# A recommendation tower: a ring of three sample tiles, hot items among the second tile's products, and nine one-hot tables instead of ten

## The chip, the core and the metric

The kernel runs on one core of a Trainium2 chip. The metric is device time in microseconds of one execution. TensorE multiplies (PE; its weight loads are listed as PEld), VectorE (DVE) and ScalarE (ACT) copy and convert, GpSimd (POOL) issues the gathers, SyncE (SP) issues most other transfers.

## What is computed

For 2048 samples, 26 embedding rows of 128 numbers are looked up, each by its id in its own table. Seven tables have 1000 rows, ten 1250, eight 12500 and one 125000. With the dense row of the sample this makes 27 vectors; all 351 products of two of them, and the dense row behind them, go through three layers:

```python
e = jnp.stack([tbl_0[ids[:, 0]], ..., tbl_25[ids[:, 25]]], axis=1)
combined = jnp.concatenate([e, r_dense_x[:, None, :]], axis=1)
z = jnp.einsum('bfd,bgd->bfg', combined, combined)[:, _TRIU_I, _TRIU_J]
h = jnp.concatenate([z, r_dense_x], axis=1)
h = jnp.maximum(h @ W_top1 + b_top1, 0.0)
h = jnp.maximum(h @ W_top2 + b_top2, 0.0)
y = h @ W_top3
```

## The kernel before

The samples are worked through in 8 blocks of 256, each of two tiles of 128 samples. In `xt` (128 embedding elements on the partitions, samples and 32 feature slots along them) a block's vectors come together; it has room for one block.

**Cold tables.** Sixteen tables are gathered (POOL, line 388): one indirect DMA for each tile and table, 128 rows into `raw`, which has two buffers, so a tile's gather waits until the tile two before it is turned. Gathers go out in bursts of three (`BURST`), and a burst waits until the first two of the burst before have landed. TensorE turns them (`turn_rows`, line 405) in four groups of four tables into an `x_ps` bank, and ScalarE copies the bank into `xt` (line 561).

**Hot tables.** The ten smallest (seven of 8 chunks of 128 rows, three of 10) lie in SBUF, split into a rounded part `hot_hi` and a residue `hot_lo`. An item is one hot table for one block; it is cut into pieces of up to 5 chunks. VectorE makes the one-hot matrix of a piece by comparing ids with row numbers (`make_piece`, line 593) into a ring of three, TensorE multiplies each chunk by `hot_hi` and `hot_lo` (`hot_piece`, line 418, 256 columns, a rounded f32 type), and ScalarE copies the finished item into `xt` (line 530). While the tables arrive, ScalarE rounds each (line 523) and VectorE makes its residue (line 582). SP loads a table when the residue of the one four before it is made, and the wide list of ids of an item (128 copies of 256 ids) when the pieces of the item four before are made.

**Products of features.** `products(m)` (line 434), called gram or G below: eight fills for each tile, each four f32 products of 108 columns (two records each in the profile), in two banks that are copied by ScalarE and VectorE together (line 269). A tile's first fill waits for the last turn of the tile and for all hot items of the block.

**Tail.** For each block: `cols` (transposes of `gram`, copied to `z`), `zt` (transposes of `z`), `h1`, `h2`, `y`: the layers, in steps of two products (lines 459 to 495).

**The order** is written out once, as a list of steps that TensorE, ScalarE and VectorE all follow. `plan(h)` (line 110) gives a block: hot pieces from the third item on, the tail steps of the block before spread among them by the costs in `COVER`, and the first tile's turns; then the first tile's fills with the second tile's turns between them; then the second tile's fills with the next block's first two items (`EARLY`) after every second fill. Those two are copied to `xt` when it is free. The last block's tail stands alone. Five weight matrices are rounded and split (lines 571 and 613) beside fills 1, 3, 5, 7 and 9.

## Time and profile before

| | us |
|---|---|
| three runs | 480.33, 480.82, 482.65; median 480.82 |
| the profiled execution | 486.82 |
| its span, first to last instruction | 485.0 |
| TensorE products busy | 437.1 (90%) |
| VectorE busy | 310.4 (64%) |
| ScalarE busy | 230.2 (47%) |
| POOL busy | 247.8 (51%) |

The span cut into 40 equal slices; a digit is the busy share of a slice in tenths, PEclk the granted clock in tenths of full speed:

```profile
PE   1776669899998999999889999999999999999978
DVE  4998237875387735885469645885488745882441
PEclk9999679999999999999999999999999999999999
DMA  6789212322123312232122321232133312310000
```

Matmuls overlap in the pipeline, so the length of a record (some 280 ns) is longer than what it costs; the cost is the distance between two starts. The engines' idle time counts only where the engine is on the way to the end.

### The profile page before, as it was taken

Reading aid. Unit: us, or ns where it says so; the run is one execution under the profiler, and the core shown is the slowest. Engines: PE = TensorE matmul, PEld = TensorE weight load, DVE = VectorE, ACT = ScalarE, POOL = GpSimd, SP = SyncE. Lnnn points to the kernel's source line nnn. Section 1 sums busy time; section 2 is a strip of 40 time slices with the busy share of each in tenths; the row PEclk is TensorE's granted clock in tenths of the full one; section 3 lists DMA queues with packets and bytes.
Section 4 is the critical chain, followed back from the end, with each engine's and each line's share of the span. In section 5 each row is a group of like instructions: output and inputs, shape, how many; then the busy total and the mean of one; then the engine's idle time right before and its main releaser. Section 6 shows DMA issues by size and latency. Waiting matters only on the chain.

```text
span 485.0 us, 9121 instructions
## 1 busy us (share of the span) xinstructions
PE 437.1 (90%) x3464; PEld 413.9 (85%) x3464; DVE 310.4 (64%) x503; ACT 230.2 (47%) x731; POOL 247.8 (51%) x264
## 2 busy tenths in 40 slices
PE   1776669899998999999889999999999999999978
PEld 1665669899897999999889998989898989889966
DVE  4998237875387735885469645885488745882441
ACT  2643343644455453644545444644546453634643
POOL 3652665655655556455654656555565556461000
PEclk9999679999999999999999999999999999999999
DMA  6789212322123312232122321232133312310000
GB/s 229 222 258 160 57 45 58 81 70 72 48 63 75 81 51 57 70 82 73 44 66 78 73 65 55 70 76 78 39 72 80 80 55 56 72 49 18 1 1 0
DMA packets 23995, 36.20 MB, mean 75 GB/s; under 512 B 6185, under 2 KB 18097, under 8 KB 23952
## 3 DMA queue, kind: packets, MB, share of 16 engines
q1 hardware_dynamic: 14880, 18.03, 14.7%
q0 software_dynamic: 8192, 16.79, 12.8%
q10 hardware_dynamic: 880, 0.80, 0.5%
q8 instruction: 28, 0.46, 0.4%
q14 instruction: 15, 0.12, 0.1%
HBM read 35.59 MB, written 0.01 MB: 73 GB/s over the span
## 4 chain that ended last, share of the span: by engine, by line
PE 82%; DMA 7%; issue 4%; POOL 3%; DVE 2%; ACT 0%; POOLq 0%; ACTq 0%; DVEq 0%
PE x_ps L418 31%; PE gram_ps L434 24%; PE tail_ps L489 15%; DMA raw<-in_tbl,ids_sb 7%; PE x_ps L405 5%; POOL raw L388 3%; PE tail_ps L468 3%; PE tail_ps L459 2%; PE tail_ps L495 2%; DVE gram L269 1%; DVE onehot L593 1%; DMA ids_sb<-in_ids 0%; DVE z L278 0%; ACT gram L269 0%; DVE zt_lo L326 0%
## 5 line engine op out<-in xcount | busy, mean ns | idle before, releaser
L388 POOL DMA_INDIRECT raw<-in_tbl,ids_sb x256 | 246.9, 964 | 190.9 <-DMA raw<-in_tbl,ids_sb 94.6
L593 DVE TENSOR_TENSOR onehot<-ids_wide,row_ps 128x1024 fp32r<-128x1024 int32 (+1 forms) x160 | 202.6, 1298 | 41.2 <-PE x_ps L418 32.3
L418 PE MATMUL x_ps<-onehot,hot_hi 128*128 128x256 f32 x688 | 180.1, 297 | 22.2 <-DVE onehot L593 20.2
L418 PE MATMUL x_ps<-onehot,hot_lo 128*128 128x256 f32 x688 | 171.4, 283 | 0.0
L418 PEld LDWEIGHTS x_ps<-onehot,hot_hi 128*128 128x128 f32 x688 | 131.3, 191 | 26.5 <-issue 11.9
L434 PE MATMUL gram_ps<-xt 128*128 128x108 f32 x1024 | 134.2, 284 | 7.3 <-DVE gram L269 5.8
L434 PEld LDWEIGHTS gram_ps<-xt 128*128 128x128 f32 x1024 | 126.9, 199 | 13.6 <-ACT gram L269 7.6
L418 PEld LDWEIGHTS x_ps<-onehot,hot_lo 128*128 128x128 f32 x688 | 131.6, 191 | 0.0
L269 DVE COPY gram<-gram_ps 32x104 f32<-32x104 f32 x256 | 68.6, 268 | 90.2 <-PE gram_ps L434 86.3
L269 ACT COPY gram<-gram_ps 32x104 f32<-32x104 f32 x256 | 60.2, 235 | 88.7 <-PE gram_ps L434 80.1
L530 ACT COPY xt<-x_ps 128x256 f32<-128x256 f32 x80 | 50.4, 633 | 50.1 <-PE x_ps L418 42.0
L405 PE MATMUL x_ps<-ident,raw 128*128 128x128 f32 x256 | 39.9, 280 | 9.3 <-issue 3.9
L561 ACT COPY xt<-x_ps 128x512 f32<-128x512 f32 x64 | 38.4, 600 | 13.8 <-PE x_ps L405 12.4
L405 PEld LDWEIGHTS x_ps<-ident,raw 128*128 128x128 f32 x256 | 30.5, 146 | 10.3 <-issue 8.6
L302 ACT ACTIVATE h_hi<-tail_ps,b_sb 128x256 fp32r<-128x256 f32 x32 | 15.2, 474 | 37.7 <-PE tail_ps L489 28.9
L489 PE MATMUL tail_ps<-zt_hi,weights_hi 118*128 118x256 f32 (+2 forms) x96 | 31.5, 353 | 0.0
L278 ACT COPY z<-tail_ps 64x104 f32<-64x104 f32 (+12 forms) x195 | 26.4, 209 | 6.3 <-PE tail_ps L459 3.9
L331 DVE TENSOR_TENSOR h_lo<-h,h_hi 128x256 fp32r<-128x256 f32 x32 | 13.7, 428 | 24.4 <-ACT h L303 15.7
L489 PE MATMUL tail_ps<-zt_hi,weights_lo 118*128 118x256 f32 (+2 forms) x96 | 25.6, 291 | 0.0
L468 PE MATMUL tail_ps<-ident,z 64*118 64x64 f32 (+3 forms) x128 | 14.8, 240 | 6.0 <-issue 2.9
L489 PE MATMUL tail_ps<-dense_sb,w1d_sb 128*128 128x256 f32 x64 | 19.9, 393 | 0.0
L468 PEld LDWEIGHTS tail_ps<-ident,z 64*118 64x118 f32 (+3 forms) x128 | 10.5, 139 | 10.8 <-issue 5.2
(36 smaller groups left out, 279.0 us busy)
## 6 DMA issues: line engine op xcount, KB each, us to landing
ids_wide<-in_hot_ids SPq DMA_DIRECT2D x80, 128.0 KB
raw<-in_tbl,ids_sb POOLq DMA_INDIRECT x256
hot_in<-in_tbl SPq DMA_DIRECT2D x7, 512.0 KB, 6.8
hot_in<-in_tbl SPq DMA_DIRECT2D x3, 640.0 KB, 6.6
dense_sb<-in_dense_t ACTq DMA_DIRECT2D x6, 128.0 KB
weights_in_place<-in_w SPq DMA_DIRECT2D x1, 512.0 KB
dense_sb<-in_dense_t SPq DMA_DIRECT2D x2, 128.0 KB
weights_in_place<-in_w SPq DMA_DIRECT2D x1, 256.0 KB
```

The costliest lines, as they stand in the source:

```text
L269: last = copy(gram[rows, :, per_fill * i:per_fill * (i + 1)], src)
L278: last = copy(z[rows, :, pair_start[q]:pair_start[q] + feats - 1 - q], src)
L302: nc.scalar.activation(h1_hi[:, j, :], ps[:, 0:BLOCK], ACT.Relu, bias=bias).then_inc(h1_rounded, 1)
L388: nc.gpsimd.indirect_dma_start(out=raw[k][:, f, :], out_offset=None, in_=tables[f], in_offset=bass.IndirectOffsetOnAxis(ap=ids_sb[:, t, f: ...
L405: last = nc.tensor.transpose(ps[:, c * P:(c + 1) * P], raw[k][:, f, :], ident[:, :])
L418: last = nc.tensor.matmul(ps, table[:, chunk_at[j] + c, :], onehot[:, p % RING, c - a, :], start=(c == 0 and table is hot_hi), stop=(c == ...
L434: last = nc.tensor.matmul(gram_ps[m % 2][:, col:col + QUAD * feats], xt[:, b:b + QUAD, :].rearrange("p b f -> p (b f)"), xt[:, b:b + QUAD, ...
L468: last = nc.tensor.transpose(ps[0:of.stop - of.start, s * groups_block:(s + 1) * groups_block], z[rows, s, of], ident[rows, rows])
L489: last = nc.tensor.matmul(ps[:, 0:BLOCK], weights, moving, start=(n == 0), stop=(n == len(products_of) - 1))
L530: copy(xt[:, :, nf + j], x_ps[fill_no["hot", it] % len(x_ps)][:, 0:BLOCK]).then_inc(x_copied, 1)
L561: copy(xt[:, b:b + P, fs[0]:fs[-1] + 1], src).then_inc(x_copied, 1)
L593: nc.vector.tensor_tensor(onehot[:, p % RING, 0:n, :], ids_wide[:, it % IDS, :].unsqueeze(1).to_broadcast([P, n, BLOCK]), row_no[chunks[it ...
```

## The change

It has several parts. `HOT` is 9: one 1250-row table goes over to the gathers, so a tile has 17 gathers in five groups of 3, 3, 4, 3 and 4. `xt` is a ring of three tiles (`XT`); `to_xt` makes a copy in two where it wraps around. Items of block 0 are for one tile each, later ones for a block; a piece holds up to 1024 columns of one-hot matrix (`PIECE`), so 8 chunks of one tile are one piece, and 4 chunks of a block. The 10-chunk items become pieces of 5 and 5 for a tile, of 3, 3 and 4 for a block.

The order in block 0: tile 0's nine items with its turns, its eight fills with an item of tile 1 after each, tile 1's last item and turns. In later blocks: the next block's first item, which is held in its bank until the first tile's products have been made; the first tile's eight fills; the second tile's turns among the item pieces that follow; then the second tile's eight fills with one hot piece after each; then the remaining items with the turns of the next first tile. The tail of a block is spread from the end of its second tile's fills to the start of the next block's. Among fills VectorE makes one piece per step, none before the first. SP loads with two tables ahead instead of three (`LOADS_AHEAD`), and four more id lists stand before the weights in its queue. The weight splits stand at fills 11 to 15. `h1_lo` takes the place of `h1`.

```diff
-HOT = 10
+HOT = 9
 RAW = 2
 DENSE = 2
 RING = 3
-PIECE = 5
-EARLY = 2
+PIECE = 4
 BURST = 3
+XT = 3
+ROUNDS_AHEAD = 2
 COVER = {"cols": 2.0, "zt": 1.0, "h1": 0.2, "h2": 0.15, "y": 0.25}
 COVER_STAGE = 2.5
 COVER_START = 1.5
-TAIL_OVER = 3
-LOADS_AHEAD = 3
+LOADS_AHEAD = 2
...
-    items = blocks * nh
+    items = [(j, t, 1) for t in range(tiles_block) for j in range(nh)]
+    items += [(j, h * tiles_block, tiles_block) for h in range(1, blocks) for j in range(nh)]
     pieces, item_end = [], []
-    for it in range(items):
-        n = chunks[it % nh]
-        count = -(-n // PIECE)
-        cut = [i * n // count for i in range(count + 1)]
+    for it, (j, _, n) in enumerate(items):
+        count = -(-chunks[j] * n * P // (PIECE * BLOCK))
+        cut = [i * chunks[j] // count for i in range(count + 1)]
         pieces += [(it, cut[i], cut[i + 1]) for i in range(count)]
         item_end.append(len(pieces))
     item_start = [0] + item_end[:-1]
...
+    last_item = [max(it for it, (_, first, n) in enumerate(items) if first <= t < first + n) for t in range(tiles)]
+    def hot_pieces(t):
+        of = [p for p, (it, _, _) in enumerate(pieces) if items[it][1] == t]
+        return [[("hot", p)] for p in of]
+    def with_turn(slots, t, ends):
+        for g in range(n_turn):
+            slots[ends[-(-(g + 1) * len(ends) // n_turn) - 1]].append(("turn", t, g))
+        return slots
+    def item_ends(slots):
+        return [i for i, slot in enumerate(slots) if slot[-1][0] == "hot" and slot[-1][1] + 1 in item_end]
+    def gram_slots(t, hot=()):
+        return [[("gram", t * n_gram + i)] + [step for slot in hot[i * len(hot) // n_gram:(i + 1) * len(hot) // n_gram]
+                                              for step in slot] for i in range(n_gram)]
...
+    slots = hot_pieces(0)
+    slots = with_turn(slots, 0, item_ends(slots)[-n_turn:])
+    tail_from, tail_to = [], []
+    for h in range(blocks):
+        t = h * tiles_block
+        hot = hot_pieces(t + tiles_block) if h + 1 < blocks else []
+        if h == 0:
+            second = hot_pieces(1)
+            slots += gram_slots(t, second[:n_gram])
+            rest_slots = second[n_gram:]
+            slots += with_turn(rest_slots, t + 1, item_ends(rest_slots))
+            lead = 0
+        elif hot:
+            held = item_end[pieces[hot[0][0][1]][0]] - hot[0][0][1]
+            slots += hot[:held] + gram_slots(t)
+            slots[-1].append(("held", pieces[hot[0][0][1]][0]))
+            lead = n_gram
+            ends = item_ends(hot[held:lead])[:-1]
+            slots += with_turn(slots[-1:] + hot[held:lead], t + 1, [0] + [end + 1 for end in ends])[1:]
+            tail_to.append(len(slots))
+        else:
+            slots += gram_slots(t) + with_turn([[] for g in range(n_turn)], t + 1, list(range(n_turn)))
+            lead = 0
+            tail_to.append(len(slots))
+        slots += gram_slots(t + 1, hot[lead:lead + n_gram])
+        tail_from.append(len(slots))
+        if hot:
+            rest_slots = hot[lead + n_gram:]
+            slots += with_turn(rest_slots, t + tiles_block, item_ends(rest_slots))
+    held_items = [step[1] for slot in slots for step in slot if step[0] == "held"]
...
+            before.setdefault(tail_from[h] + min(int(at * n / span[-1]), n - 1), []).append(("tail", h, key, part))
+        for i, steps in before.items():
+            slots[i][:0] = steps
+    order = [step for slot in slots for step in slot]
...
+        for n, step in enumerate(order):
             if step[0] == "hot":
                 used = step[1]
             end = min(used + RING + 1, len(pieces))
+            coming = [s[0] for s in order[n + 1:] if s[0] in ("gram", "hot")][:1]
+            if step[0] == "gram":
+                end = min(end, nxt + 1)
+            elif coming == ["gram"]:
+                end = nxt
...
-        xt = sb("xt", [P, BLOCK, SLOTS])
+        xt = sb("xt", [P, XT * P, SLOTS])
...
-        onehot = sb("onehot", [P, RING, PIECE, BLOCK], F32R)
+        onehot = sb("onehot", [P, RING, PIECE * BLOCK], F32R)
...
-        h1 = sb("h1", [P, m1, BLOCK])
...
+        with nc.sbuf_tensor("h1", [P, m1, BLOCK], F32) as h1:
+            pass
...
+        weights_at_gram = range(gram_block - len(weight_parts), gram_block)
...
+        def to_xt(copy, first, n, feature, src):
+            at = first % XT
+            runs = [(0, n)] if at + n <= XT else [(0, XT - at), (XT - at, n)]
+            for a, b in runs:
+                place = (first + a) % XT * P
+                last = copy(xt[:, place:place + (b - a) * P, feature], src[:, a * P:b * P])
+            return last
...
-                if j == EARLY:
-                    dense_load(0)
+            dense_load(0)
+            for it in range(nh, nh + IDS):
+                ids_load(it)
...
-                h, i = divmod(m, gram_block)
-                if i % n_gram == 0:
-                    t = h * tiles_block + i // n_gram
-                    pe.wait_ge(x_copied, max(fill_no["turn", t, n_turn - 1], fill_no["hot", h * nh + nh - 1]) + 1)
-                    pe.wait_ge(dense_copied, h + 1)
+                t, i = divmod(m, n_gram)
+                if i == 0:
+                    pe.wait_ge(x_copied, max(fill_no["turn", t, n_turn - 1], fill_no["hot", last_item[t]]) + 1)
+                    pe.wait_ge(dense_copied, t // tiles_block + 1)
                 for done in (gram_act, gram_dve):
                     reach(pe, done, m - 1)
                 for g in range(per_fill):
-                    b = (i * per_fill + g) * QUAD
+                    b = t % XT * P + (i * per_fill + g) * QUAD
...
-                if j == 0:
+                to_xt(copy, first, n, nf + j, x_ps[fill_no["hot", it] % len(x_ps)]).then_inc(x_copied, 1)
+                if j == nh - 1 and first % tiles_block == 0:
+                    h = first // tiles_block
                     act.wait_ge(dense_in[h % DENSE], (h // DENSE + 1) * 16)
-                    copy(xt[:, :, nf + nh], dense_sb[h % DENSE][:, :]).then_inc(dense_copied, 1)
-
-            for j in range(EARLY):
+                    to_xt(copy, first, tiles_block, nf + nh, dense_sb[h % DENSE]).then_inc(dense_copied, 1)
+            for j in range(ROUNDS_AHEAD):
...
-                    if what[0] + 1 == item_end[it]:
-                        if it >= nh and it % nh < EARLY:
-                            waiting.append(it)
-                        else:
-                            hot_copy(it)
-                elif kind == "xt free":
-                    if waiting:
-                        act.wait_ge(gram_full, (what[0] + 1) * gram_block)
-                    for it in waiting:
+                    if what[0] + 1 == item_end[it] and it not in held_items:
                         hot_copy(it)
-                    waiting = []
+                elif kind == "held":
+                    hot_copy(*what)
...
+                    if what[0] in weights_at_gram:
                         act.wait_ge(weights_in, n_weights * 16)
-                        hi, _, src = weight_parts[what[0] // 2]
+                        hi, _, src = weight_parts[weights_at_gram.index(what[0])]
                         copy(hi, src).then_inc(weights_rounded, 1)
```

## Rows read from the trace of the kernel before

**Rows 1.** Busy time by stretch: PE, PEld, DVE, ACT, POOL, granted clock, DMA share, GB/s.

```profile
0.00:48.50 48.50, 27.35 (x188) 24.62 (x188) 40.45 (x36) 20.29 (x26) 22.17 (x26) 1.00 0.80 217
48.50:72.80 24.30, 16.31 (x87) 15.57 (x88) 7.23 (x20) 9.02 (x25) 15.87 (x17) 0.70 0.19 51
72.80:485.00 412.20, 393.42 (x3191) 373.75 (x3189) 262.74 (x448) 200.93 (x682) 209.73 (x222) 0.99 0.23 59
```

**Rows 2.** Who TensorE waited for, 120 to 450 us: us in total, times, longest.

```profile
PE gram_ps L434 <- DVE gram L269: 5.8, 9, 1.2
PE x_ps L418 <- DVE onehot L593: 3.0, 2, 1.6
```

**Rows 3.** Chain that ended last, from the page: shares of the span by engine.

```profile
PE 82%; DMA 7%; issue 4%; POOL 3%; DVE 2%; ACT 0%; POOLq 0%; ACTq 0%; DVEq 0%
```

**Rows 4.** Timeline of POOL's gathers: start, length in us, instruction, idle before and releaser.

```profile
12.16 1.43 POOL L388 DMA_INDIRECT raw<-in_tbl,ids_sb  x1 [5.49 <-DMA raw<-in_tbl,ids_sb]
...
19.42 0.97 POOL L388 DMA_INDIRECT raw<-in_tbl,ids_sb  x1 [2.43 <-DMA raw<-in_tbl,ids_sb]
...
43.07 0.94 POOL L388 DMA_INDIRECT raw<-in_tbl,ids_sb  x1 [0.30 <-issue]
...
48.54 0.95 POOL L388 DMA_INDIRECT raw<-in_tbl,ids_sb  x1 [3.27 <-DMA raw<-in_tbl,ids_sb]
...
53.03 0.94 POOL L388 DMA_INDIRECT raw<-in_tbl,ids_sb  x1 [1.04 <-DMA raw<-in_tbl,ids_sb]
```

**Rows 5.** Timeline of VectorE in the first stage, one table and the next.

```profile
11.55 1.22 DVE L582 TENSOR_TENSOR hot_lo<-hot_in,hot_hi 128x1024 fp32r<-128x1024 f32 x1
12.69 2.35 DVE L593 TENSOR_TENSOR onehot<-ids_wide,row_ps 128x1024 fp32r<-128x1024 int32 x2
14.95 1.22 DVE L582 TENSOR_TENSOR hot_lo<-hot_in,hot_hi 128x1024 fp32r<-128x1024 f32 x1
```

**Rows 6.** Timeline of TensorE in the first stage: transposes, first fill, fills at 70.60.

```profile
22.95 0.60 PE L405 MATMUL x_ps<-ident,raw 128*128 128x128 f32 x4
...
49.00 1.14 PE L434 MATMUL gram_ps<-xt 128*128 128x108 f32 x8 [0.68 <-ACT xt L561]
...
70.60 4.38 PE L434 MATMUL gram_ps<-xt 128*128 128x108 f32 x24
```

**Rows 7.** Timeline of TensorE, one-hot products of a steady block, ten intervals apart.

```profile
251.07 0.28 PE L418 MATMUL x_ps<-onehot,hot_lo 128*128 128x256 f32 x1
...
252.27 0.28 PE L418 MATMUL x_ps<-onehot,hot_lo 128*128 128x256 f32 x1
```

**Rows 8.** DMA issues of one list of ids and one table, from the page.

```profile
ids_wide<-in_hot_ids SPq DMA_DIRECT2D x80, 128.0 KB
...
hot_in<-in_tbl SPq DMA_DIRECT2D x3, 640.0 KB, 6.6
```

**Rows 9.** TensorE: nine fills, small transposes with their group's mean, unrounded and rounded products.

```profile
260.95 0.44 PE L468 MATMUL tail_ps<-ident,z 64*118 64x64 f32 x4
...
L468 PE MATMUL tail_ps<-ident,z 64*118 64x64 f32 x32 | 3.4, 225 | 3.6 <-issue 2.9 <-ACTq L293 0.6
...
456.16 8.48 PE L434 MATMUL gram_ps<-xt 128*128 128x108 f32 x72
...
477.05 0.60 PE L489 MATMUL tail_ps<-dense_sb,w1d_sb 128*128 128x256 f32 x2
...
477.60 0.28 PE L489 MATMUL tail_ps<-zt_hi,weights_lo 118*128 118x256 f32 x1
```

**Rows 10.** Groups of equal shape: line, engine, operation, busy us, mean ns, idle before.

```profile
L593 DVE TENSOR_TENSOR onehot<-ids_wide,row_ps 128x1024 fp32r<-128x1024 int32 x112 | 132.2, 1218 | 31.8 <-PE x_ps L418 27.4 <-issue 3.7
...
L269 DVE COPY gram<-gram_ps 32x104 f32<-32x104 f32 x256 | 68.6, 268 | 90.2 <-PE gram_ps L434 86.3 <-issue 0.7
...
L561 ACT COPY xt<-x_ps 128x512 f32<-128x512 f32 x64 | 38.4, 600 | 13.8 <-PE x_ps L405 12.4 <-remote 0.8
...
L613 DVE TENSOR_TENSOR weights_lo<-weights_in_place,weights_hi 128x512 fp32r<-128x512 f32 x3 | 2.1, 692 | 1.8 <-ACT weights_hi L571 1.8
```

87 lines of the change are left out of this document (31 added, 56 removed).

## The prediction

> **What bounds the kernel now.** I read the busy shares by stretch first [rows 1]. The span has two parts. Until 72.8 us TensorE is half empty: it works 27.4 of the first 48.5 us and 16.3 of the next 24.3. From there to the end it works 393.4 of 412.2 us, and its largest waits in 330 us of it are 5.8 us for gram copies and 3.0 us for one-hot pieces [rows 2]. So after 73 us nearly every product removed is time removed, and before it TensorE's work is worth nothing until it passes what it waits for. Next I asked what that is. The chain of waits over the whole span names TensorE for 82% and the gathers into `raw` for 7% [rows 3]; the gather's own rows show two stages: bursts of three, 7.3 us from one to the next while tables are loaded (12.16 to 19.42), 4.5 us from 48.5 us on [rows 4]. VectorE is full in the same first stage: one residue and two one-hot pieces for each 1000-row table, 3.40 us a table [rows 5]. The first product stage starts at 49.00, when tile 0's 16th gather is in. The second tile's products (G8) start inside the group of 24 records at 70.60; its first third is G7, so G8 is at about 71.9 [rows 6]. That moment divides the sum: up to it the gathers decide, behind it TensorE.
>
> **What changes, by part.** I wrote out both orders from the code. (a) Nine hot tables: a steady block has 76 chunks for 86, 152 one-hot products for 172, and 17 gathers and 5 turn groups per tile for 16 and 4. (b) Block 0's hot items are made per tile, 128 columns wide. Tile 0's products no longer wait for tile 1, and tile 1's hot work stands between them. (c) Steady blocks: the next block's first item, eight fills of the first tile with the previous block's tail between them, its turns late, then eight fills with a hot piece after each. (d) The five weight splits move from G1, G3 ... G9 to G11 ... G15. (e) Three tile slots of `xt`; a copy that wraps around (blocks 1, 4 and 7) is made in two.
>
> *Hot products behind G8.* Blocks 1 to 7, 20 fewer in each: 140. Ten intervals of a stream take 1.20 us [rows 7], the same in the first stage at full clock [rows 6]; with 0.119 us each, -16.7 us. The pieces are 20 per block before and after, so their start cost stays.
>
> *Transposes and groups.* Tiles 2 to 15 turn one more feature and one more group. Four transposes take 0.60 us, of which the last one's own length is some 0.28, so one costs (0.60 - 0.28)/3 = 0.107 us: 14 x 0.107 = 1.5. A new group costs TensorE a break of some 0.1 us [rows 6 and 7]: 1.4. Together +2.9.
>
> *When G8 starts.* Two things must be there. First the gathers. Tile 0 now needs the 17th, which is the second of the sixth burst (43.07 us, in before 48.54) [rows 4]. Up to 48.5 us the DMA moved 217 GB/s, 10.5 MB [rows 1]. The change takes one table of 640 KB and half of ten lists of 128 KB (0.64 MB) out of this [rows 8]; four more lists of 64 KB come in, and the weights, over 1 MB, are issued behind the ninth item instead of beside it, of which I count a third. About 1.4 MB less stands ahead of that burst: 6.5 us. So it lands at about 42 and the first products start at 43. Bounds: 49.3 if nothing is saved; and 38, where tile 0's hot work ends when a table takes VectorE two operations instead of three (2.27 us, 2.9 for 1250 rows) at the pace of the loads, about 3 us [rows 5]. Second, TensorE from there: eight fills of 0.93 (72 records, nine fills, in 8.48 with the last one's length [rows 9]) are 7.4, tile 1's turns 17 x 0.107 and five breaks with the last copy 2.9, and 152 products of 128 columns at a price p. No row has p. From below: a transpose of 64 columns with a 118-column weight load beside it takes (0.44 - 0.225)/3 = 0.07 us, so the load alone does not hold a product longer; from above: a product of unrounded f32, two records, takes 0.43 us for 256 columns (477.05 to 477.60 less one rounded product), so 0.215 for 128, and the gram's 0.231 for 108 columns would scale to 0.27 [rows 9]. I take 0.107, the row of the same width: 16.3. Then G8 = 43 + 7.4 + 16.3 + 2.9 = 69.6. The gathers for it: the 34th is first of the twelfth burst, six steps of 4.45 behind the sixth (35.5), so issued at 62 to 67 and landed by 69. Both meet at 70: G8 comes 2.3 us earlier (bounds 7 earlier, 4 later at this p).
>
> The Trainium skill (TensorE: Matmul & The Clock Gate, LDWEIGHTS) says a load costs its columns over 1.2 GHz, 107 ns for 128, whatever the products; by it a narrow product would cost as much as a wide one and p could not be under 0.107. The rows speak against that floor, since 118 columns were loaded every 0.07 us [rows 9]. By the one G8 would be 69.6, by the other 64, where the gathers would decide; the forecast hardly moves.
>
> *The clock.* TensorE is granted 0.70 between 48.5 and 72.8, part of it at 1.2 GHz, after waits of 1 to 2 us between short groups; from 72.8 on it is 0.99 [rows 1]. The three fills at 70.60 took 4.38 us [rows 6], where nine later ones take 8.48 [rows 9], so 1.5 us too long; two thirds of it lie behind G8. With tile 1's hot work filling the gaps it should be at 2.4 GHz: -1.0.
>
> *Weight splits.* In before they lay in a stage that waited for gathers, so they were free. Now each (0.69 us on VectorE [rows 10]) meets a gram copy pair of 0.55 and a piece of 1.22 in a step in which TensorE needs 0.93 + 1.04 = 1.97: VectorE has 2.46. Five times 0.5, less what three pieces in store absorb: +2 (0 to 3).
>
> *VectorE and ScalarE in steady blocks.* Without the split a step with a fill and a piece costs VectorE 0.55 + 1.22 and some 0.1 of latency [rows 10], 1.87 against 1.97: it just holds. ScalarE has less there. Around the `cols` stages both orders give ScalarE about as much work as TensorE, so I let the short waits there stay as they are.
>
> *Waits in steady blocks.* Gram waits between 120 and 450 are 5.8 us, 1 a block [rows 2]; they come where turn copies of 0.60 [rows 10] sit before gram copies on ScalarE. After the change no turn stands among fills, so up to 8 us in the whole span go; new are three turn groups in a row with copies of 0.5 to 0.6 behind each (0.5 a block), and the last block, where `cols` copies are pressed into few slots (2). Part of the new ones falls into time that was lost anyway. Net -3 (none gone and 4 new at one end, -8 at the other).
>
> *At nothing.* The gathers of the later tiles: 34 per block at 4.45 per three are 50.4 us, against a block of 55 now and about 52 after; POOL is up to two tiles ahead. Tightest is tile 2: its last gather is in the 17th burst, five steps behind the twelfth, landed by 92; its turn stands 32 us behind G8 (eight steps of 1.97, 44 chunks at 0.24, breaks and `cols`), at 102. If that cover goes, it costs the difference, some us in block 1. The wrapped copies: 27 more short copies on ScalarE, which idles for half of the span. Narrow id lists: SP, off the path. h1_lo in the place of h1: same operations.
>
> **The sum.** -2.3 - 1.0 - 16.7 + 2.9 + 2.0 - 3.0 = -18.1. On the profiled execution 485.0 becomes 466.9; that execution took 486.8 in all and the three runs 480.3 to 482.7, median 480.8, so the forecast for the median is 480.8 - 18.1 = 462.7. Its own range, adding the bounds of G8 (-7 to +4), splits and waits not all at one end: 455 to 472.
>
> **Rivals.** *Narrow products cost like unrounded f32.* For: no row shows a rounded product under 256 columns, and it is the width at which its 0.119 us lies just above the transposes of half the columns. Against: transposes of 128 and 64 columns get cheaper with their width. It is charged twice, as tile 0's hot work no longer fits either: G0 = 10.65 + 152 p + 2.9, G8 = G0 + 7.4 + 152 p + 2.9 = 23.85 + 304 p. The remaining terms are -15.8, so the change turns into a loss from G8 = 87.7, p = 0.210. With p = 0.23 G8 is 93.8, +21.9 - 15.8 = +6.1: 487 (482 at 0.215, 499 at 0.27). This is the one on the other side.
> *VectorE cannot hold the alternation.* If its step is 2.1 rather than 1.87, it sets the pace of eight steps in each block: 0.13 x 64 = 8.3, and the -3 is not had either: +11.3 on the forecast, 474. For: 0.1 us of room. Against: three pieces in store.
> *The start gains nothing:* loads with two ahead instead of three starve the first tables, G0 stays at 49: G8 75.9, 469.
> *The new order does not do what it says:* fills wait as before and the clock stays low between 49 and 73 (no -3, no -1.0): 467. It lies in the forecast's range and is counted there.
>
> **Chances.** Forecast with its neighbours at the start and the waits (455 to 472) 0.57; below 455 0.04; VectorE or ScalarE (472 to 478) 0.10; narrow products dear 0.29, of which slower than 483 0.19, within 0.5% 0.07, still faster 0.03. The rival's 0.27 end is less likely than 0.23, so 489 leaves about 0.10 above and 0.04 below: 455 to 489. Half a per cent, 2.4 us, is about what a measurement of this kernel can tell. Faster 0.73, same 0.08, slower 0.19.
>
> **What would show it.** Spacing of `onehot` products of block 0: 0.07 to 0.12 or above 0.2. G0 near 43, G8 near 70 with the clock at full in between. One-hot products 1064 of 256 columns and 304 of 128. Gram waits of half of now; a VectorE wait between G11 and G15; turns waiting for `raw` only in the first two blocks. The forecast is wrong if G8 is later than 76 or a steady block stays above 53.5 us.

## The result, and the profile after

The change makes the kernel slower: 505.25 us (504.21 to 507.03) against 481.74 (480.33 to 486.86), ratio 1.047 [1.039, 1.056]. The forecast was 462.7 (455 to 489). The profiled execution took 504.21 us, with a span of 502.2. Ratios here and below are of undisturbed executions beside those of the kernel before on the same chip, with a 95% interval; times without a ratio can come from different chips.

The slices of the page look better than before, TensorE 467.9 us busy (93%):

```profile
PE   1999999997999999999999999999897998989978
DVE  4763323289855984598459845975477545922251
PEclk9999999999999999999999999999999899976999
DMA  5746422223422331334132213322233222111000
```

They mislead. The chain of what ended last, by engine and by line, is led by another engine than in before [rows 3]:

```profile
DMA 53%; issue 19%; POOL 16%; PE 10%; ACT 1%; POOLq 0%; DVE 0%; ACTq 0%; DVEq 0%
DMA raw<-in_tbl,ids_sb 52%; POOL raw L437 16%; PE tail_ps L537 4%; PE gram_ps L482 4%; PE tail_ps L516 1%; DMA ids_sb<-in_ids 0%; PE tail_ps L543 0%; PE x_ps L454 0%; POOLq L436 0%; ACT xt L604 0%; PE tail_ps L507 0%; DVE z L326 0%; ACT y_sb L356 0%; ACT gram L317 0%; DVE zt_lo L374 0%
```

In before TensorE made 82% of it and the gathers 7%. Now 88% of it is gathers: their flight (52%), their issue on POOL (16%), and "issue" (19%), here the 0.30 us between two of a burst and the 0.7 to 0.9 us from a landing to the first gather of the next burst. POOL waits in this trace for landings (151.3 us) and for "issue" (55.2), and never for a buffer that TensorE has still to turn, so the pace of the gathers is their own. Its timeline, in the middle and at the end (columns as in [rows 4]):

```profile
311.56 0.94 POOL L437 DMA_INDIRECT raw<-in_tbl,ids_sb  x1 [2.25 <-DMA raw<-in_tbl,ids_sb]
312.80 0.95 POOL L437 DMA_INDIRECT raw<-in_tbl,ids_sb  x1 [0.30 <-issue]
314.05 0.95 POOL L437 DMA_INDIRECT raw<-in_tbl,ids_sb  x1 [0.30 <-issue]
316.74 0.95 POOL L437 DMA_INDIRECT raw<-in_tbl,ids_sb  x1 [1.74 <-DMA raw<-in_tbl,ids_sb]
...
467.37 0.94 POOL L437 DMA_INDIRECT raw<-in_tbl,ids_sb  x1 [1.13 <-DMA raw<-in_tbl,ids_sb]
468.62 1.16 POOL L437 DMA_INDIRECT raw<-in_tbl,ids_sb  x1 [0.30 <-issue]
```

A burst of three takes 5.2 us here, and the mean is 5.0: from the ninth burst (59.25) to the 91st (467.37) there are 82 steps of 4.98. The last gather goes out at 468.62, 33.6 us before the end; at the 2.7 us from issue to landing that the page gives it has landed by some 471, and what stands behind it (a turn group, eight fills, a tail of a block) takes the 31 us to 502.2. TensorE waits little for it in any one place. From 120 to 450 us:

```profile
PE x_ps L454 <- DMA raw<-in_tbl,ids_sb: 6.3, 3, 3.6
PE tail_ps L516 <- DVEq L376: 3.1, 5, 0.6
PE x_ps L454 <- ACT xt L604: 2.7, 2, 1.6
PE x_ps L467 <- DVE onehot L638: 0.8, 1, 0.8
PE gram_ps L482 <- ACT xt L604: 0.8, 1, 0.8
```

The 6.3 us of waits for `raw` are all after 334 us. The 5.8 us of gram waits [rows 2] are gone. Windows of the stages (columns of [rows 1]):

```profile
10.70:98.20 87.50, 85.86 (x402) 85.09 (x402) 38.51 (x47) 23.97 (x52) 44.76 (x45) 1.00 0.45 114
98.20:235.18 136.98, 133.25 (x1093) 128.21 (x1093) 100.87 (x161) 72.20 (x254) 76.37 (x81) 1.00 0.31 67
...
334.00:471.00 137.00, 126.85 (x995) 121.05 (x996) 72.61 (x138) 66.55 (x237) 79.75 (x84) 0.94 0.24 57
```

In the last of them the granted clock is down too, 0.94 after 1.00, so the late gathers cost more than the 6.3 us of waits.

In the first TensorE is 98% busy for 87 us, with what the forecast's prices make 47 us of work (304 products at 0.107, fills 7.4, turns and breaks about 7). G8 starts at 98.20, where the forecast had 69.6 and before 71.9 [rows 6]. TensorE's timeline there, and from the groups of equal shape that of the narrow products:

```profile
11.20 0.41 PE L467 MATMUL x_ps<-onehot,hot_hi 128*128 128x128 f32 x1
11.41 0.41 PE L467 MATMUL x_ps<-onehot,hot_lo 128*128 128x128 f32 x1
...
98.20 2.04 PE L482 MATMUL gram_ps<-xt 128*128 128x108 f32 x8 [0.80 <-ACT xt L604]
...
100.29 0.41 PE L467 MATMUL x_ps<-onehot,hot_lo 128*128 128x256 f32 x1
100.50 0.41 PE L467 MATMUL x_ps<-onehot,hot_hi 128*128 128x256 f32 x1
...
103.06 0.28 PE L467 MATMUL x_ps<-onehot,hot_hi 128*128 128x256 f32 x1
103.18 0.28 PE L467 MATMUL x_ps<-onehot,hot_lo 128*128 128x256 f32 x1
```

```profile
L467 PE MATMUL x_ps<-onehot,hot_hi 128*128 128x128 f32 x152 | 63.6, 419 | 10.7 <-DVE onehot L638 10.7
```

Narrow products start 0.2135 us apart, all of them, and a fill of eight records takes 2.04 where it takes 1.03 later. The same rows show wide products at 0.21 apart at 100.3 and at 0.12 at 103.1. So up to about 101.7 us everything on TensorE runs at half rate, the lower of the two levels (1.2 GHz), although the granted clock reads 1.00 in the window. Behind that a block that doesn't wait for gathers takes 50.37 us (235.18 to 285.55) against 54.7 before; from 330 us on two of them take 53 and 57.

So two things went wrong: the start lost 26 us on TensorE, and in this trace the gathers set the end. The experiments ask which of them counts.

### The profile page after: what moved, and what is told of

Its sections match the earlier page's. It is cut to its first block, busy times and chain, and to the rows that moved or that the text cites. A ratio compares the mean times of both kernels' runs of the same rounds, so it can differ in the third digit from the quotient of the medians.

```text
span 502.2 us, 9214 instructions
## 1 busy us (share of the span) xinstructions
PE 467.9 (93%) x3472; PEld 448.1 (89%) x3472; DVE 293.4 (58%) x504; ACT 232.3 (46%) x777; POOL 261.1 (52%) x280
## 4 chain that ended last, share of the span: by engine, by line
DMA 53%; issue 19%; POOL 16%; PE 10%; ACT 1%; POOLq 0%; DVE 0%; ACTq 0%; DVEq 0%
DMA raw<-in_tbl,ids_sb 52%; POOL raw L437 16%; PE tail_ps L537 4%; PE gram_ps L482 4%; PE tail_ps L516 1%; DMA ids_sb<-in_ids 0%; PE tail_ps L543 0%; PE x_ps L454 0%; POOLq L436 0%; ACT xt L604 0%; PE tail_ps L507 0%; DVE z L326 0%; ACT y_sb L356 0%; ACT gram L317 0%; DVE zt_lo L374 0%
## 5 line engine op out<-in xcount | busy, mean ns | idle before, releaser
L437 POOL DMA_INDIRECT raw<-in_tbl,ids_sb x272 | 260.2, 956 | 207.9 <-DMA raw<-in_tbl,ids_sb 151.3
L467 PE MATMUL x_ps<-onehot,hot_hi 128*128 128x256 f32 (+1 forms) x684 | 205.4, 326 | 13.7 <-DVE onehot L638 13.7
L638 DVE TENSOR_TENSOR onehot<-ids_wide,row_ps 128x1024 fp32r<-128x1024 int32 (+2 forms) x162 | 183.2, 1153 | 47.3 <-PE x_ps L467 44.5
L467 PE MATMUL x_ps<-onehot,hot_lo 128*128 128x256 f32 (+1 forms) x684 | 196.0, 312 | 0.0
L467 PEld LDWEIGHTS x_ps<-onehot,hot_hi 128*128 128x128 f32 x684 | 151.9, 222 | 18.2 <-issue 13.3
L467 PEld LDWEIGHTS x_ps<-onehot,hot_lo 128*128 128x128 f32 x684 | 152.1, 222 | 0.0
L299 ACT COPY xt<-x_ps 128x128 f32<-128x128 f32 (+1 forms) x108 | 45.8, 477 | 84.2 <-PE x_ps L467 84.0
L604 ACT COPY xt<-x_ps 128x384 f32<-128x384 f32 (+1 forms) x80 | 47.0, 630 | 11.0 <-PE x_ps L454 10.9
L537 PEld LDWEIGHTS tail_ps<-zt_hi,weights_lo 118*128 118x128 f32 (+2 forms) x96 | 19.0, 198 | 0.9
L537 PEld LDWEIGHTS tail_ps<-zt_hi,weights_hi 118*128 118x128 f32 (+2 forms) x96 | 18.9, 197 | 1.0
```

The lines of the kernel that those rows point to most:

```text
L299: last = copy(xt[:, place:place + (b - a) * P, feature], src[:, a * P:b * P])
L437: nc.gpsimd.indirect_dma_start(out=raw[k][:, f, :], out_offset=None, in_=tables[f], in_offset=bass.IndirectOffsetOnAxis(ap=ids_sb[:, t, f: ...
L467: last = nc.tensor.matmul(ps, table[:, chunk_at[j] + c, :], columns(p)[:, c - a, :], start=(c == 0 and table is hot_hi), stop=(c == chunks ...
L537: last = nc.tensor.matmul(ps[:, 0:BLOCK], weights, moving, start=(n == 0), stop=(n == len(products_of) - 1))
L604: copy(xt[:, b:b + P, fs[0]:fs[-1] + 1], src).then_inc(x_copied, 1)
L638: nc.vector.tensor_tensor(columns(p), ids_wide[:, it % IDS, 0:width].unsqueeze(1).to_broadcast([P, n, width]), row_no[chunks[j]][:, a:b].u ...
```

## The experiments

**One table less in the old order.**

```diff
-HOT = 10
+HOT = 9
```

> The kernel before with nine one-hot tables alone (order, widths and loads as before). Theory G: the gathers set the end. In the traces they follow each other at 1.66 us each on average (80 bursts of three in 398 us before, 4.98 us a burst), not at the 4.45 us a burst that the prediction took, and the kernel ends some 31 us after the last gather has landed. 16 more gathers are 26.6 us more, so the last lands near 468 and the span is about 498. Theory C: what costs is TensorE's half rate during the 128-column products; here there are none, so my sum holds: 160 fewer one-hot products at 0.119 us, 3 us back for transposes, span 469.

Measured 502.4 us, 1.041 [1.033, 1.049], with a span of 495.5. Taking out the tenth one-hot table alone, in the old order with full-width products, gives nearly the whole loss, and Theory G holds. TensorE's waits over the span:

```profile
PE x_ps L405 <- DMA raw<-in_tbl,ids_sb: 34.3, 9, 5.2
PE x_ps L405 <- issue: 14.6, 7, 5.6
```

Its last gather is issued at 462.0. The one block without a wait for gathers still takes only 50.2 us; later ones, with turns waiting, 54 to 59:

```profile
120.00:170.20 50.20, 49.49 (x417) 47.60 (x416) 33.86 (x57) 27.78 (x92) 27.35 (x29) 1.00 0.30 65
```

**Narrow products made wide, with nine tables and with ten.** Each is streamed twice side by side, so 256 columns, and nothing else changes.

```diff
...
-                        last = nc.tensor.matmul(ps, table[:, chunk_at[j] + c, :], columns(p)[:, c - a, :],
+                        moving = columns(p)[:, c - a, :].unsqueeze(1).to_broadcast([P, copies, tiles_item * P])
+                        last = nc.tensor.matmul(ps, table[:, chunk_at[j] + c, :], moving,
...
```

> The changed kernel with block 0's narrow one-hot products made 256 columns wide by streaming the same 128 columns twice; same order, same results. TensorE should reach full rate as in the kernel before (products 0.12 us apart instead of 0.2135) and the second tile's first fill moves from 98.2 to 72 us. Theory G: this gains nothing at the end, since the gathers keep their pace: span 499 to 503. Theory C: the 26 us come off at the end too: span 476.

> The changed kernel with ten one-hot tables instead of nine, and block 0's products streamed twice as wide, so it has the new order and tile ring, 16 gathers a tile and TensorE at full rate. Theory G: the last gather lands near 442, and the end follows 31 us later or after TensorE's own work (50.4 + 2.0 us a block from 72 us on), so 473 to 478, less than both kernels. Theory C gives 476 to 480. A span above 485 would speak against both: the new order itself would then cost.

With nine tables 508.2 us, 1.056 [1.050, 1.063]: G8 comes at 79.4 instead of 98.2, 19 us earlier (72 was expected), and nothing of it reaches the end: the span is 507.0. Its chain has 56% of gathers in flight and TensorE waits for `raw` 31.1 us. With ten tables, so 256 gathers, the same kernel takes 486.5 us, 1.012 [1.007, 1.017]. Its span of 483.9 is above both expectations (473 to 480) and hardly under the 485 that would have spoken for a cost of the new order; that cost comes up again below. In block 0 twice the columns, most of them at the full level, are faster than half of them at the lower one; and 16 gathers fewer, with the tenth table's products added, make 22 us.

**The 17th gather left out.** The rest of the change stays; the 17th cold table's rows aren't read and its feature takes the 16th's vectors. Then the same with wide products.

```diff
...
-                    for f in fs:
-                        n = t * nf + f
+                    for f in [f for f in fs if f < gathered]:
+                        n = t * gathered + f
...
```

> The changed kernel without the gather of the last of the 17 cold tables (its features are those of the 16th table); TensorE, ScalarE and VectorE do the same work. Theory G: 16 gathers fewer, the last lands near 444 instead of 471, and TensorE's own work sets the end: G16 at 137, then 50.4 us a block: span 484 to 489. Theory C: gathers do not matter, span 502.

> The changed kernel without its 17th gather and with block 0's products streamed to 256 columns: both suspected costs taken away in another manner. Without the gather alone the span was 488.1 with the second tile's first fill at 97.8; with wide products that fill stood at 79.4. If both causes add up as I say: 488.1 - 18.4 = 470. If the half rate in block 0 was recovered anyway later: 480 to 488.

490.0 us, 1.018 [1.012, 1.023], a span of 488.1 as Theory G had it, with no wait for `raw` at all and TensorE 89% of the chain. This is what the narrow products cost when gathers don't hide them: G8 is at 97.8, 26 us later than before, blocks of 50.38 give 4.3 back each, and the two nearly cancel: a span of 488.1 against 485.0. With wide products 476.9 us, 1.003 [0.997, 1.009], G8 at 77.8 and a span of 471.1 (470 was expected). The two ran on different chips: by the ratios the narrow form costs 1.5%, by the spans 17 us. In the second trace the gathers end the kernel again (DMA 47%, "issue" 17%, POOL 14% of the chain, the last one issued at 437.75, 33.3 us before the end), so this isn't yet all that the narrow form costs TensorE. Even without the 17th gathers and with most of the clock back the changed kernel gains nothing against the kernel before.

**The new order without the narrow products.** Items of block 0 full width, the second tile's turns among the first tile's fills, with ten and with nine tables. The tile ring, the smaller pieces, the loads two ahead and the late weight splits stay as in the changed kernel.

```diff
...
-            second = hot_pieces(1)
-            slots += gram_slots(t, second[:n_gram])
-            rest_slots = second[n_gram:]
-            slots += with_turn(rest_slots, t + 1, item_ends(rest_slots))
+            slots += with_turn(gram_slots(t), t + 1, list(range(n_gram)))
...
```

> The changed kernel with ten one-hot tables and block 0's items 256 columns wide for both tiles at once, as before the change; kept are the new order of the steady blocks, the tile ring and the held item. A steady block took 52.2 us with ten tables and this order, 54.7 before. Theory G: 16 gathers a tile, the last lands near 442 and the earliest end is 473; TensorE has the second tile's first fill near 72 to 74 us, then seven blocks at 2.5 us less: span 485 - 17 + 1 = 467 to 474, so the gathers or TensorE end it, 2 to 3% faster than before. Rival: the new order gains in a block only what it loses at the seams, span 482 to 486.

> The same with nine one-hot tables and 17 gathers a tile. TensorE has the least work of all these kernels. Theory G: still 272 gathers at 1.66 us, span 496 to 503. Theory C (narrow products at half rate are the cost): none here, span 460 to 466.

490.8 us, 1.017 [1.011, 1.023] with ten and 505.9, 1.049 [1.041, 1.058] with nine. The first is slower than either of its expectations (a span of 490.0; 467 to 474, or 482 to 486), the second close to Theory G's 496 to 503 (503.7). So the order, with the ring and what else came with it, costs 1.7%, nine tables cost 15 us on top, and with both the result is the change's. Which part of the order costs this wasn't taken apart. With nine tables TensorE waits 25.7 + 12.2 us in front of turns.

**Is it a clock that was never granted?** Five wide f32 products on nothing ahead of the first item.

```diff
+            for n in range(5):
+                nc.tensor.matmul(tail_ps[0][:, :], ident[:, :], ident[:, :].unsqueeze(1).to_broadcast([P, 4, P]),
+                                 start=True, stop=True)
```

> The changed kernel with five unrounded f32 products of 512 columns on TensorE before the first one-hot product, in time in which it waits; their output is not used. It asks what a 128-column product costs once the engine runs at full rate, and whether the rate stays. If narrow products are slow by themselves they stay 0.2135 us apart; if it was the clock they start 0.06 to 0.12 us apart. The gathers set the end either way: span 499 to 505.

One execution: 501.0 us, G8 at 98.7. The products' starts, the windows on both sides, and TensorE between there and G8, here and in the changed kernel (last row):

```profile
16.35 0.28 PE L467 MATMUL x_ps<-onehot,hot_lo 128*128 128x128 f32 x1
16.46 0.27 PE L467 MATMUL x_ps<-onehot,hot_hi 128*128 128x128 f32 x1
...
18.19 0.45 PE L467 MATMUL x_ps<-onehot,hot_hi 128*128 128x128 f32 x1 [0.67 <-DVE onehot L641]
18.44 0.41 PE L467 MATMUL x_ps<-onehot,hot_lo 128*128 128x128 f32 x1
18.65 0.41 PE L467 MATMUL x_ps<-onehot,hot_hi 128*128 128x128 f32 x1
...
9.00:18.00 9.00, 5.92 (x48) 5.58 (x48) 8.23 (x8) 4.70 (x7) 3.20 (x3) 0.97 0.73 238
18.00:30.00 12.00, 11.81 (x57) 11.84 (x57) 8.90 (x9) 5.42 (x10) 4.44 (x5) 0.50 0.76 253
...
48.00:98.70 50.70, 49.90 (x233) 49.50 (x233) 16.11 (x27) 10.12 (x30) 29.81 (x32) 0.50 0.25 63
...
47.50:98.20 50.70, 49.90 (x233) 49.50 (x233) 16.12 (x27) 10.17 (x30) 25.87 (x28) 1.00 0.36 74
```

This execution shows one thing more. TensorE has no wait put down to `raw` in it (one in front of a turn, of 3.1 us up to 46.16, has the releaser "issue") and makes 89% of its chain, the last gather is issued at 461.5, and the span is 499.0 all the same, with steady blocks of 50.6 to 53.3 us. In the changed kernel the two ends, of the gathers and of TensorE, lie close together.

**Do the id lists slow the gathers?** Only the first four wide lists of ids are moved; later items compare with stale ids.

```diff
...
-                reach(sp, piece_ready, item_end[it - IDS] if it >= IDS else 0)
+                if it >= IDS:
+                    return
...
```

> The changed kernel without the transfers of the wide id lists after the first four (later items compare with the first four lists, so the looked-up rows are others). In its trace bursts of gathers beside which 450 to 520 KB moved took 5.7 to 6.0 us, those with 200 KB 4.5 to 4.9. If the lists delay the gathers, the mean burst falls from 4.98 to about 4.6 to 4.7 us, the last gather lands 22 to 30 us earlier and TensorE ends the kernel at 486 to 490. If the gathers are slow for another reason, span 500 to 503.

504.0 us, 1.048 [1.041, 1.055], but the burst's mean falls from 5.0 to 4.7 us and the last gather goes out at 443.0, nearly 26 us earlier. So the lists' transfers do lengthen bursts. The end doesn't follow, against what I expected: its profiled execution has a span of 496.8 and steady blocks of 50.4 to 54.1 us, with short TensorE waits whose releaser the trace calls "issue". I can't say where they come from. This run speaks on the bursts; on the end it says that earlier gathers alone don't always bring it forward.

**Bursts of six.** POOL issues six gathers before it waits, waits are merged by semaphore, and the room for descriptors is doubled. In the changed kernel, in the new order at full width with nine tables, and in the old order with nine tables:

```diff
-BURST = 3
+BURST = 6
...
+                            leads = {}
...
-                                pool.wait_ge(lead_in[tl % RAW][group_of[fl]], landed(tl, group_of[fl], False, fl))
+                                leads[tl, group_of[fl]] = fl
+                            for (tl, gl), fl in leads.items():
+                                pool.wait_ge(lead_in[tl % RAW][gl], landed(tl, gl, False, fl))
...
-    nc = bacc.Bacc("TRN2", target_bir_lowering=False, num_devices=1, dynamic_dma_scratch_size=4096)
+    nc = bacc.Bacc("TRN2", target_bir_lowering=False, num_devices=1, dynamic_dma_scratch_size=8192)
```

> The changed kernel with gathers issued in bursts of six instead of three (a burst still waits for all but the last gather of the one before), nothing else of the work changed. In its trace a burst of three is 1.25 us to the start of the second gather, 2.5 us until that has landed, 0.85 us to the next burst: 4.6, and 5 on the mean, 1.66 us a gather. Six give 5.0 + 2.5 + 0.85 = 8.4, with the mean's excess 8.8, 1.46 us a gather. Theory G: the last gather lands near 420 to 430, and TensorE's work ends the kernel, as in the kernel without the 17th gather: span 486 to 491. If the DMA engines and not the waits between bursts set the pace, span 500 to 503.

> The changed kernel with block 0's items for both tiles at once (256 columns, as before) and bursts of six. Gathers are no longer the bound, no product is narrow, nine tables: TensorE has the second tile's first fill at 72 to 77 us and 50.4 us a block: 488 less 21 to 26 us: span 462 to 467. This is my forecast's number, reached only once both faults of its reasoning are taken away. Rival: stalls on TensorE take the room, span 475 to 485.

> The kernel before with nine tables and bursts of six, its own order. Alone, nine tables gave a span of 495.5. Theory G: now TensorE's sum holds, 485 - 19 + 3 = 469, with the weight of the order change being the difference to the kernel above. If nine tables are no gain on TensorE either: 480 or more.

488.0 us, 1.037 [1.027, 1.047]; 459.3 us, 0.969 [0.944, 0.994]; 446.0 us, 0.946 [0.937, 0.954]. The last gathers go out at 425.0, 401.3 and 414.6 us in place of 468.6, 468.6 and 462.0, and waits for `raw` are left only in the first 120 us, in the changed kernel none. These three ran on one chip, on which the kernel before took 476.5 us, 5 less than in the first comparison; so the changed kernel's time falls by 17 us, but its ratio only from 1.047 to 1.037. Its trace has a span of 486.0 (486 to 491 was expected) and the blocks of 50.38 of the kernel without the 17th gathers (488.1). On this one chip the full-width block 0 is worth 28.7 us more (488.0 to 459.3, G8 at 67.4 instead of 97.8), and the old order another 13.3 (459.3 to 446.0).

The second kernel's 459.3 us is the place where the forecast's 462.7 is reached: once the gathers are faster and no product is narrow. The third was expected at a span of 469 and has 445.1; I had counted with the long blocks of the trace of before, and they weren't there. It is the fastest kernel of all. Its POOL timeline at one of the shortest bursts, and the window of one block:

```profile
299.61 0.94 POOL L391 DMA_INDIRECT raw<-in_tbl,ids_sb  x1 [1.85 <-DMA raw<-in_tbl,ids_sb]
300.85 0.95 POOL L391 DMA_INDIRECT raw<-in_tbl,ids_sb  x1 [0.30 <-issue]
...
305.84 0.94 POOL L391 DMA_INDIRECT raw<-in_tbl,ids_sb  x1 [0.30 <-issue]
308.08 0.94 POOL L391 DMA_INDIRECT raw<-in_tbl,ids_sb  x1 [1.29 <-DMA raw<-in_tbl,ids_sb]
```

```profile
208.94:258.41 49.47, 49.41 (x418) 47.59 (x417) 33.88 (x57) 27.78 (x92) 29.82 (x32) 1.00 0.29 70
```

These six take 8.47 us. The mean from the ninth burst (85.83) to the last (413.37) is 8.85, or 1.48 us a gather, where the same kernel with bursts of three has 4.89, or 1.63. DMA moves 70 GB/s here and 65 in the block of the kernel with bursts of three above, so it was the wait for the burst before, not bandwidth, that set the pace. TensorE is busy 49.41 of 49.47 us.

**How much of it is the bursts alone?** The kernel before with bursts of six, and the changed kernel with them and wide products.

> The kernel before with bursts of six gathers and nothing else: ten hot tables, 256 gathers, the old order. Theory A, the old order never waits for gathers after 73 us, so the bursts only bring the start forward: the first fill of tile 0 at 45 and of tile 1 at 68 (as with nine tables and bursts of six) in place of 49.0 and 71.9, and blocks stay at 54.7 us, so the time falls by 4 us against the kernel before, ratio 0.99. Then 31 of the 36 us of the nine-table kernel with bursts of six are the tenth table's products and the waits they bring. Theory B, the old order is itself paced by gathers in a way that its waits hide: blocks fall towards 52 us (49.5 plus twenty products of 0.12), so 7 x 2.7 = 19 us more, ratio 0.95, and the tenth table is worth 17 us, the forecast's term.

> The changed kernel with bursts of six gathers and the 128-column products of block 0 streamed twice, so 256 columns wide. Theory: with the gathers out of the way the narrow products' half clock is the rest of the loss; the first fill of tile 1 comes at 78 in place of 97.8 us, so the time falls by 19 to 20 us from the 488.0 us of the changed kernel with bursts of six alone: 468 to 469 us, ratio 0.98 to 0.985. Rival: gathers set the end again as soon as the start is early: their last is issued by 425 us, so the end could be no later than 425 + 3 + 31 = 459 us from them, and they cannot hold it; if the time stays above 480 us another wait has taken the place, and the spacing of products in block 0 or a new wait for raw would show it.

Neither expectation held: 593.7 us, 1.205 [1.197, 1.212], and 621.1 us, 1.259 [1.251, 1.267], on a chip on which the kernel before took 492.0. In the first, the fill of 156.46 on TensorE, the two engines that copy it and POOL:

```profile
156.46 2.01 PE L437 MATMUL gram_ps<-xt 128*128 128x108 f32 x8 [2.33 <-DVE gram L269]
...
162.20 0.55 DVE L269 COPY gram<-gram_ps 32x104 f32<-32x104 f32 x2 [5.88 <-remote]
...
162.20 0.48 ACT L269 COPY gram<-gram_ps 32x104 f32<-32x104 f32 x2 [5.95 <-remote]
...
160.59 0.95 POOL L391 DMA_INDIRECT raw<-in_tbl,ids_sb  x1 [0.31 <-issue]
```

The fill ends at 158.5, and both copies start together 3.7 us later, after POOL's burst (its last gather ends at 161.5). Two late pairs before it, at 147.83 and 155.77, start inside a burst, so the end of the burst isn't what they wait for. The trace has no releaser for it ("remote"). Three more runs, on another chip, ask whether this belongs to the kernel, the chip or the room for descriptors:

> The kernel before with bursts of six gathers, once more, on another draw of a chip. Its first measurement was 593.7 us against 492.0 of the kernel before, where two theories had 477 or 458; in it VectorE's and ScalarE's copies started up to 3.7 us after TensorE's last product of the group had ended, while GpSimd issued gathers without a pause. Theory A, the delay belongs to kernels with bursts of six on the chip of that measurement: here the time is 455 to 480 us. Theory B, it belongs to this kernel (bursts of six beside the order of fills and turns of ten hot tables): above 560 us again.

> The nine-table kernel in the old order with bursts of six, once more: 446.0 us before. Theory A, the delay goes with the chip: beside a ten-table kernel that is fast here it is 446 us again; if the chip is such a one, both are slow, this one above 530 us. Theory B, the delay goes with the kernel: 446 us whatever the other does.

> The kernel before with the room for the descriptors of GpSimd's transfers doubled to 8192 bytes, bursts of three as before. If that room is what brings the delay, this kernel is slower than the kernel before by 50 us or more wherever the two others are slow; if it is the longer burst alone, the time is the kernel before's within 0.5%.

462.6 us, 0.981 [0.969, 0.992]; 449.8 us, 0.952 [0.938, 0.965]; and 473.7 us, 0.994 [0.987, 1.001] for the room alone. The same kernel took 593.7 us on one chip and 462.6 on another, so the delay goes with the chip (or its state at the time), and bursts of six are exposed to it where bursts of three, at 492.0 us on the same chip, were hardly. One execution of the kernel before, on the chip of the first bursts of six, took 616.8 us where the twelve others took 470 to 481; whether that is the same trouble isn't known. What holds the copies back stays open, and whether the 446 us kernel would be slow on the bad chip wasn't tried.

With ten tables and bursts of six a block takes 52.1 us (167.28 to 219.37), TensorE busy for 52.03 of it:

```profile
167.28:219.37 52.09, 52.03 (x435) 50.16 (x434) 36.55 (x60) 26.89 (x91) 34.00 (x37) 1.00 0.31 74
```

Against 49.5 with nine that is 2.6 us for twenty products and two pieces, near the forecast's 2.4. And against the 54.7 of the trace before it is 2.6 less, with the order unchanged. The run with the larger room and bursts of three has blocks of 52.1 too (174.08 to 226.16), and no gram waits. Nor has the first experiment, with nine tables and the room unchanged (50.2). So those waits in the trace of before [rows 2] weren't a property of its order; they come and go between traces, and what brings them isn't shown.

## Why the prediction was wrong

**The failed step: "At nothing. The gathers of the later tiles: 34 per block at 4.45 per three are 50.4 us."** I took one of the shortest bursts for the mean. [rows 4] shows 4.49 between the two bursts at 48.5 and 53.0, and I priced the 85 behind the sixth by it; the same timeline has the last of the 256 gathers at 438.50, and from 48.54 that is 79 steps of 4.94. With 5.0 the 34 gathers of a block take 56.7 us, more than a block. From the forecast's own sixth burst (35.5) 85 steps of 5.0 are 425: the last gather leaves at 462, lands near 465, and with 31 us behind it the kernel ends near 495, outside the range (from the 37.79 at which that burst did begin, 498). All numbers for this were in the trace of before, whose last eight fills begin near 457 and whose span ends at 485, 28 us later; a turn group and its copy in front of them make it some 31. "POOL is up to two tiles ahead" names the room, and it hid nothing: the room is a fixed store, and a rate that is too low empties it, here by about 330 us, where turns begin to wait. I looked for the tightest place in tile 2; the turns that waited were those of the last tiles. In before the same sum gives 441 + 31 = 472 against 485, so gathers had 13 us of room, and 16 more at 1.66 use 27. The table that left TensorE (2.4 us a block) went to the queue that had less room than it took. The runs bear this out from both sides: 16 gathers fewer, or a faster pace, and TensorE ends the kernel at spans of 488.1 and 486.0; 272 gathers at the old pace, and it is 495 to 507 with every order and width tried. What stays open is the run without id lists (last gather at 443.0, span 496.8), where the earlier gathers didn't bring the end forward.

**Second, the clock: "With tile 1's hot work filling the gaps it should be at 2.4 GHz: -1.0."** It came out the other way. The price p = 0.107 at the full level was right (0.111 measured in the run with wide products ahead). But the sum for G8 took the clock as given, and p at the lower level, 0.2135, is the rival's number: its G8 = 23.85 + 304 p gives 88.8, and 98.2 was measured since fills and turns ran at half rate too. Its threshold, a loss from p = 0.210, was passed. The rival's arithmetic was nearly right with the wrong mechanism; what I argued against it (smaller products get cheaper with their width) says nothing about the level. That the measured 505 lies beyond its 482 to 499 is no credit to it either: its cause alone gives a span of 488. The early rows of before already show it: its first fourteen wide products are 0.21 apart too, up to 13.6 us, then 0.12; there it lasted 3 us. Here the 26 us at G8 are nearly hidden behind the gathers, as the wide form shows.

The Trainium skill (TensorE: Matmul & The Clock Gate, LDWEIGHTS) puts a load of 128 columns at 107 ns, its columns over 1.2 GHz. In the prediction I set rows of 118-column loads every 0.07 us against it. As a floor for the distance of these products the traces agree with the page at the full level: 0.111 for 128 columns beside 0.119 for 256. At the lower level both widths took 0.2135, twice the page's figure.

**What held.** The gathers for G0: the 17th goes out at 39.04, so it is in by 42, as forecast. G0 itself is at 47.5 instead of 43 because TensorE was behind. Hot products 0.119 each and a tenth table's 20 per block: 2.6 us a block measured for 2.4. The transposes and groups: no run takes them apart. VectorE's alternation: no wait for a piece over 0.8 us from 120 us on, so that rival is out. Weight splits: +2 (0 to 3) was right. Beside them, from 112 to 120 us, TensorE waits four times for a piece, 3.0 us in all, as the signs to look for had it. The longest, and the split in front of the piece that it waits for:

```profile
115.54 0.69 DVE L658 TENSOR_TENSOR weights_lo<-weights_in_place,weights_hi 128x512 fp32r<-128x512 f32 x1
...
117.63 0.36 PE L467 MATMUL x_ps<-onehot,hot_hi 128*128 128x256 f32 x1 [1.44 <-DVE onehot L638]
```

**The waits, "Net -3".** Gram waits did go, as forecast, but the runs with ten tables show that they also go without the change. So part of the 485.0 that I subtracted from was a loss of that one execution. In their place the new order has 3.1 us of waits at the transposes of `z`, and its block is 50.38 where the old order with the same nine tables has 49.47. "The new order does not do what it says" was a rival at 467 with no price for a loss; without the narrow products the order costs 1.7% with ten tables and, with nine and bursts of six, 13.3 us.

**The verdicts of the rivals.** The one that ended on the slow side named the right place, the start, and a cause that doesn't decide: taken away, it leaves 508 us. No rival had the gathers as the bound behind 73 us; the section that costed them at nothing saw at most "some us in block 1". The range ended at 489 for that reason. Of the signs named, G8 later than 76 came, and so did turns waiting for `raw` long after the first two blocks.

## What to carry to other kernels

Before you cost a stream of transfers at nothing, take its mean pace from first to last over the whole trace, multiply by the new count and add the work behind the last one: that end has to lie before TensorE's. A busy TensorE isn't a fast one: compare the distance between two starts of the same shape early and late before you trust a busy share or a granted clock. And a queue that waits for "the burst before" can be set by that wait and not by bandwidth; more in flight (1.63 to 1.48 us a gather) was worth more than any order of the products, but try such a change on more than one chip. And use the mean here too: one burst picked from a timeline is what misled the forecast.

## What the runs showed of the hardware that I had not expected

At the full level 128-column products with a weight load each start 0.111 us apart. TensorE was at the lower level after 48 of them with gaps between (0.2135 from then on), and 80.5 us with 75.8 of work on them, fills and turns didn't bring it back. In the changed kernel the full level came at about 101.7 us, behind the first piece of 256-column products. The granted clock reads 1.00 ahead of the first change of level in the changed kernel and in before, with products 0.21 us apart.

An id list moving beside gathers lengthens a burst: without the lists its mean is 4.7 us in place of 5.0, at 45 against 66 GB/s.

On one of the chips copies started 3.7 us after the product that they waited for, in a kernel in which POOL issues six gathers in a row, and a kernel of 462 us took 594.
